# Layer 0 attention: products with v two steps behind their scores and between the halves of a step, scores in steps without items one head at a time

## The chip, the cores and the metric

The kernel runs on one core of one Trainium2 chip. The metric is the device time of one execution in microseconds. Engines are named as in the profile: PE is TensorE (PEld its weight loads), DVE VectorE, ACT ScalarE, POOL GpSimd, SP the queue that issues DMAs.

## The reference, cut to what matters

```python
x = L0_attn_x                                   # [2, 1024, 128]
xn = layernorm(x)
x = x + attn0(xn) + ffn0(xn)                    # layer 0
xn = layernorm(x)
x = x + attn1(xn) + ffn1(xn)                    # layer 1 (linear attention by chunks, gated LoRA)

def attn0(x):                                   # 16 heads of width 8
    q, k, v = split(x @ W_attn + b_attn)
    att = q @ k.T / sqrt(8)
    att = att + (tril(j - i) + causal) * slope[h]
    att = softmax(att)
    return (att @ v) @ W_proj + b_proj
```

Only the attention of layer 0 is touched by the change. Layer 1 follows it and takes the second half of the time.

## The kernel before, in words

The 2 x 16 heads of layer 0 are worked off in 8 groups of 4 heads (`GROUPS`, `GH = 4`). A group has 10 units (`UNITS`, `NU = 10`), so there are 80 steps (`NSTEP`); step s is unit u = s mod 10 of group n = s // 10. In what follows S0 to S3 are the scores of the four heads of a step, e0 to e3 their exponentials, A and B the items of the first and second half of a step, and pv(s) the products with v of step s.

A step's **scores** (`scores`, L706) are matmuls of the operands `k_op` and `q_op`, 55 rows deep, up to 512 columns wide. Even heads use the upper half of the rows of PE and odd heads the lower half. Each head's scores go into one of three PSUM banks in turn (`ST_BANKS = 3`), so S of a head waits until the exponential three heads earlier is done: S3 waits for e0 of its own step, S0 of the next step for e1, S1 for e2. ACT takes the **exponential** of each head (L1485) into `prob`, which has three slots, one for each step (`P_SLOTS`). On a step with a diagonal block (units 0, 1, 2, 3, 8, 9) POOL then clears the upper triangle (L1625). Then PE makes the **products with v** (`pv`, L724), four heads side by side in strips of 16 columns, into PSUM bank 7. Units 2 and 9 end an accumulation; ACT copies bank 7 to `yacc` (`acc`, L1474), and the pv of units 3 and 0 wait for that copy (`s_acc`). Units 1 and 8 have two segments (384 and 128 columns), units 2 and 9 only 256 columns.

Beside this stand the **items**, work for later groups, put into steps by `items_of_step`. A "max" item is a set of score matmuls without the maximum subtracted (L594, here called M), with a mask added in some of them (L608), whose row maxima DVE takes (L1174). Its matmuls are put beside those of the scores in the same half of a step (`scores_beside`), one in the upper, one in the lower half of the rows. Items use two rings of PSUM banks in turn, so an item waits until the one two before it has been used (`s_used`). Most steps have two max items, one in each half. Once in steps of units 1 and 5 the first half has a "turn" item (L690): PE transposes the maxima that POOL has split, ACT copies them (L1439), and SP moves them with four DMAs into `q_op` (L491). The turn at unit 1 serves the scores of unit 3 of the same group, the one at unit 5 those of unit 0 of the next. Behind the latter's DMAs the same queue loads the operands of the next but one group (`load_ops`, L483), which the max item in unit 9 needs. From step 70 on there are no max items left; steps 71, 72, 73 and 76 have one other item each, that of step 76 being the transposes of the second layer norm (L683).

The order is written out by hand for every engine, and each engine works strictly in that order. Before the change pv(s-1) stood at the end of step s on PE, and `acc(s-1)` at the end of step s on ACT.

Of the kernel before, what the change touches and what calls it, by code (L numbers as in the profile page):

```python
# [33 lines left out]
GH = 4  # L34
# [58 lines left out]
NSTEP = NU * len(GROUPS)  # L93
# [16 lines left out]
MAX_OF = [(p, r) for rs in (range(NR0), range(NR0, NR)) for p in range(PAIRS) for r in rs]  # L110
NPART = ROWS_AT[1] + 8 * TPS
P_SLOTS = 3
ST_BANKS = 3
OP_SLOTS = 3
FIRST_ITEMS = 17
# [70 lines left out]
def build(nc, x, w, wright, consts, alibi_q, alibi_k, masks, chosen, out):  # L186
    alibi_q, alibi_k, masks, chosen = (v.bitcast(BF16) for v in (alibi_q, alibi_k, masks, chosen))
    with ExitStack() as ctx:
# [353 lines left out]
        def _(pe):  # L542
# [150 lines left out]
            def scores(s, heads):  # L693
                n, u = divmod(s, NU)
                slot = n % OP_SLOTS
                if u in (0, 3) and heads[0] == 0:
                    pe.wait_ge(s_mop[n % 2][int(u == 3)], 16 * GH * (n // 2 + 1))
                for h in heads:
                    k = GH * s + h
                    if k >= ST_BANKS:  # L700
                        pe.wait_ge(s_exp, k - ST_BANKS + 1)
                at = 0
                for j, i0, nn in UNITS[u][1]:
                    for h in heads:
                        rows = rows_of(h, EXP_K)
                        last = mm(PS[:, (GH * s + h) % ST_BANKS, at:at + nn], k_op[rows, slot, h // 2, P * j:P * j + P],  # L706
                                  q_op[rows, slot, h // 2, P * i0:P * i0 + nn], start=True, stop=True, skip_group_check=True)
                        if at + nn == UNIT_W[u]:
                            last.then_inc(s_st, 1)
                    at += nn  # L710
# [62 lines left out]
                for part in range(2):  # L773
                    unit_b(k, part)
            pe.wait_ge(s_unit_used, len(UB))
            for s in range(NSTEP + 1):
                beside = items_of_step(s) if s < NSTEP else ()
                for half in range(2):
                    mine = (beside[:(len(beside) + 1) // 2], beside[(len(beside) + 1) // 2:])[half]
                    if s < NSTEP:  # L780
                        heads = range(GH // 2 * half, GH // 2 * (half + 1))
                        if mine and ITEMS[mine[0]][0] == "max":
                            scores_beside(s, heads, mine[0])
                            mine = mine[1:]
                        else:
                            scores(s, heads)
                    for k in mine:
                        item(k)
                if s:
                    pv(s - 1)  # L790


            pe.wait_ge(s_exp, GH * NSTEP)
            all_used(pe, len(ITEMS))
            pe.wait_ge(s_acc, 1 + 2 * len(GROUPS))
# [597 lines left out]
        def _(a):  # L1393
# [79 lines left out]
                        a.wait_ge(s_scr[n > 0], SCR_EACH)  # L1473
                    sca.copy(yacc[:, n, SPAN * half:SPAN * half + SPAN], PS[:, 7, :]).then_inc(s_acc, 1)  # L1474

            for s in range(NSTEP + 1):
                u = s % NU
                beside = items_of_step(s) if s < NSTEP else ()
                if P_SLOTS <= s < NSTEP:
                    a.wait_ge(s_pv, s - P_SLOTS + 1)  # L1480
                for half in range(2):
                    for h in range(GH // 2 * half, GH // 2 * (half + 1)) if s < NSTEP else ():
                        k = GH * s + h
                        a.wait_ge(s_st, k + 1)
                        sca.activation(prob[:, s % P_SLOTS, h, 0:UNIT_W[u]], PS[:, k % ST_BANKS, 0:UNIT_W[u]],  # L1485
                                       ACT.Exp).then_inc(s_exp, 1)
                    for k in (beside[:(len(beside) + 1) // 2], beside[(len(beside) + 1) // 2:])[half]:
                        item(k)
                if s:
                    acc(s - 1)  # L1490
                if s < NSPAN:
                    second(NSPAN + s)
            for i in SECOND:
# [290 lines left out]
```

## Time and profile before

| what | value |
| --- | --- |
| median of 3 runs | 516.56 us (514.7 to 519.3) |
| the profiled execution | 514.42 us, span 512.7 us |
| busy PE, DVE, ACT, POOL | 431.6, 343.4, 264.7, 197.2 us |
| steps of the loop | 44.6 us (first scores) to 291.9 us (last product with v) |
| mean granted clock of PE | 0.948 of full speed |

The profiled execution lies 2.1 us under the median. A busy share of PE is no measure of its limit, since its matmuls overlap; waits and the chain of what released what tell more.

### The profile page before, as it was taken

Reading aid. Unit: us, or ns where it says so; the run is one execution under the profiler, and the core shown is the slowest. Engines: PE = TensorE matmul, PEld = TensorE weight load, DVE = VectorE, ACT = ScalarE, POOL = GpSimd, SP = SyncE. Lnnn points to the kernel's source line nnn. Section 1 sums busy time; section 2 is a strip of 40 time slices with the busy share of each in tenths; the row PEclk is TensorE's granted clock in tenths of the full one; section 3 lists DMA queues with packets and bytes.
Section 4 is the critical chain, followed back from the end, with each engine's and each line's share of the span. In section 5 each row is a group of like instructions: output and inputs, shape, how many; then the busy total and the mean of one; then the engine's idle time right before and its main releaser. Section 6 shows DMA issues by size and latency. Waiting matters only on the chain.

```text
span 512.7 us, 10900 instructions
## 1 busy us (share of the span) xinstructions
PE 431.6 (84%) x4283; PEld 195.2 (38%) x4284; DVE 343.4 (67%) x604; ACT 264.7 (52%) x593; POOL 197.2 (38%) x285
## 2 busy tenths in 40 slices
PE   6797889898998989998886896955979888978995
PEld 3253223232332323332232252412536445544764
DVE  5868778878888788888825095648763783656351
ACT  1566387877776677768676412224523350434331
POOL 3013325353322304122220227465754846485340
PEclk9999699999999899999997598977999999999999
DMA  7543070524202020020000023211020302120000
GB/s 238 185 131 71 2 247 2 176 47 170 70 3 71 1 60 13 3 70 2 2 3 2 0 93 113 83 41 63 23 83 22 106 25 80 62 84 2 4 22 22
DMA packets 19095, 31.96 MB, mean 62 GB/s; under 512 B 2544, under 2 KB 7120, under 8 KB 18724
## 3 DMA queue, kind: packets, MB, share of 16 engines
q1 hardware_dynamic: 19044, 31.27, 19.0%
q8 instruction: 34, 0.56, 0.4%
q14 instruction: 17, 0.14, 0.1%
HBM read 13.23 MB, written 8.06 MB: 42 GB/s over the span
## 4 chain that ended last, share of the span: by engine, by line
PE 41%; DVE 27%; DMA 8%; ACT 7%; POOL 7%; issue 6%; SPq 3%; DVEq 0%; ACTq 0%; POOLq 0%
DVE pmax L1174 13%; PE PS L724 7%; PE PS L941 6%; PE PS L706 5%; PE PS L839 4%; ACT prob L1485 4%; DMA k_op<-k_scr 3%; DMA turned<-by_sin 3%; PE PS L594 3%; POOL qr L1646 3%; DVE by_sin L1321 2%; SPq L491 2%; DVE qr L1317 2%; PE PS L560 2%; PE PS L608 2%
## 5 line engine op out<-in xcount | busy, mean ns | idle before, releaser
L1174 DVE TENSOR_REDUCE pmax<-PS 128x8 f32<-128x1024 f32 x144 | 170.8, 1221 | 38.7 <-PE PS L608 29.7
L1485 ACT ACTIVATE prob<-PS 128x512 f32<-128x512 f32 (+1 forms) x320 | 158.2, 561 | 73.8 <-PE PS L706 72.6
L1625 POOL TENSOR_SCALAR_AFFINE_SELECT prob<-prob 128x512 f32<-128x512 f32 x64 | 39.9, 635 | 170.3 <-ACT prob L1485 170.3
L706 PE MATMUL PS<-q_op,k_op 55*128 55x512 bf16 (+3 forms) x384 | 93.3, 339 | 13.3 <-ACT prob L1485 10.0
L594 PE MATMUL PS<-k_op,q_op 52*128 52x512 bf16 (+3 forms) x384 | 78.9, 338 | 12.9 <-DVE pmax L1174 9.2
L724 PE MATMUL PS<-prob,vaug 128*16 128x512 f32 (+3 forms) x768 | 82.3, 518 | 1.4 <-ACT prob L1485 1.4
L839 PE MATMUL PS<-xnT,w_sb 128*128 128x512 f32 x80 | 45.8, 674 | 20.8 <-DVE by_sin L1321 20.8
L706 PEld LDWEIGHTS PS<-q_op,k_op 55*128 55x128 bf16 x384 | 26.1, 95 | 92.0 <-ACT prob L1485 74.7
L1354 DVE TENSOR_TENSOR state<-PS,xn 128x512 f32<-128x512 f32 x28 | 19.3, 691 | 54.6 <-PE PS L923 28.6
L1646 POOL TENSOR_TENSOR qr<-qr,turned 128x512 f32<-128x512 f32 x32 | 40.8, 1281 | 18.4 <-DMA turned<-by_sin 18.1
L1671 POOL TENSOR_TENSOR xn<-state,c_sb 128x512 f32<-128x512 f32 x28 | 29.1, 1041 | 41.7 <-DVE state L1354 33.5
L1552 ACT COPY oT<-PS 128x512 f32<-128x512 f32 x32 | 17.1, 587 | 39.7 <-PE PS L910 39.7
L594 PEld LDWEIGHTS PS<-k_op,q_op 52*128 52x128 bf16 x384 | 21.6, 94 | 31.1 <-DVE pmax L1174 22.4
L1517 ACT ACTIVATE vdec<-vk,c_sb 128x64 f32<-128x64 f32 x128 | 32.3, 335 | 0.5
L1506 ACT COPY vk<-PS 128x512 f32<-128x512 f32 x16 | 9.3, 584 | 42.3 <-PE PS L850 42.3
L941 PE MATMUL PS<-oT,w_sb 128*128 128x256 f32 (+1 forms) x160 | 29.2, 341 | 1.2 <-ACT oT L1552 1.2
L941 PEld LDWEIGHTS PS<-oT,w_sb 128*128 128x128 f32 x160 | 25.3, 191 | 6.7 <-issue 3.0
L1321 DVE TENSOR_TENSOR by_sin<-PS,c_sb 128x512 f32<-128x512 f32 x40 | 27.3, 681 | 0.0
L1317 DVE TENSOR_TENSOR qr<-PS,c_sb 128x512 f32<-128x512 f32 x32 | 21.9, 686 | 7.5 <-PE PS L839 7.5
L839 PEld LDWEIGHTS PS<-xnT,w_sb 128*128 128x128 f32 x80 | 13.3, 201 | 35.3 <-DVE by_sin L1321 24.6
L1328 DVE TENSOR_TENSOR sm<-PS,c_sb 128x512 f32<-128x512 f32 x32 | 20.5, 683 | 6.8 <-PE PS L868 6.8
L724 PEld LDWEIGHTS PS<-prob,vaug 128*16 128x16 f32 x768 | 14.7, 96 | 23.6 <-issue 13.6
(187 smaller groups left out, 552.3 us busy)
## 6 DMA issues: line engine op xcount, KB each, us to landing
turned<-by_sin SPq DMA_DIRECT2D x80, 128.0 KB, 2.0
k_op<-k_scr SPq DMA_DIRECT2D x14, 220.0 KB
q_op<-q_scr SPq DMA_DIRECT2D x14, 208.0 KB
c_sb<-const_dram SPq DMA_DIRECT2D x1, 2060.0 KB, 7.3
w_sb<-w_dram SPq DMA_DIRECT2D x1, 1876.5 KB, 7.6
q_scr<-part_a SPq DMA_DIRECT2D x6, 256.0 KB, 3.4
k_scr<-part_a SPq DMA_DIRECT2D x6, 256.0 KB, 3.7
q_scr<-part_b SPq DMA_DIRECT2D x6, 256.0 KB, 3.5
```

The costliest lines, as they stand in the source:

```text
L594: return mm(PS[:, ring + odd, P * at:P * (at + nb)], q_op[rows, slot, pair, P * i:P * i + P], k_op[rows, slot, pair, P * j:P * (j + nb)], ...
L706: last = mm(PS[:, (GH * s + h) % ST_BANKS, at:at + nn], k_op[rows, slot, h // 2, P * j:P * j + P], q_op[rows, slot, h // 2, P * i0:P * i0 ...
L724: last = mm(PS[STRIP * h:STRIP * h + VW, 7, c0:c0 + nn], vaug[:, TPB * b + j, g * GH + h, :], prob[:, s % P_SLOTS, h, at:at + nn], start=( ...
L839: mm(bank01(("p", i, m)), w, xnT[:, SPAN * i:SPAN * i + SPAN], start=True, stop=True).then_inc(s_pj, 1)
L941: last = mm(of_half(ps, s), wo[:, C * kt:C * kt + C], of_half(oT[:, i % 2, kt, :], s), start=False, stop=(chunks.stop == TPS and s == 1 an ...
L1174: vec.tensor_reduce(pmax[:, of_pair, at:at + TPS], both.rearrange("p a (b c) -> p a b c", c=P), AX.X, ALU.max).then_inc(done, 1)
L1317: note(vec.tensor_tensor(dst, ps, K["cos"][:, t], ALU.mult))
L1321: vec.tensor_tensor(by_sin[:, n % SIN_SLOTS, :], ps, K["sin"][:, t], ALU.mult).then_inc(free(("p", i, m)), 1)
L1485: sca.activation(prob[:, s % P_SLOTS, h, 0:UNIT_W[u]], PS[:, k % ST_BANKS, 0:UNIT_W[u]], ACT.Exp).then_inc(s_exp, 1)
L1517: sca.mul(vdec[:, c % 2, g, h % HPG, :], vk[:, c % 2, D1 * g:D1 * g + D1], K["kdec"][:, h:h + 1]).then_inc(s_vd_a, 1)
L1625: po.affine_select(out=blk, in_=blk, compare_op=ALU.is_ge, fill=0.0, base=0, pattern=[[0, GH], [1, P]], channel_multiplier=-1).then_inc(s_ ...
L1646: po.tensor_tensor(dst, dst, turned[:, n % TURN_SLOTS, :], ALU.add).then_inc(done, 1)
```

## The change

On PE the loop runs over `NSTEP + LAG` steps with `LAG = 2`. From step 2 on, pv(s-2) is issued in step s after the first half's scores and items and ahead of S2; after the last step pv(78) and pv(79) follow. On ACT `acc(s-2)` stands between e2 and e3 of step s. Where a half of a step has no max item at its head, its two heads are issued one after the other, each with its own wait for a bank, instead of both behind the wait for the later one.

```diff
+LAG = 2
@@ PE
-            for s in range(NSTEP + 1):
+            for s in range(NSTEP + LAG):
                 beside = items_of_step(s) if s < NSTEP else ()
                 for half in range(2):
+                    if half and s >= LAG:
+                        pv(s - LAG)
                     mine = (beside[:(len(beside) + 1) // 2], beside[(len(beside) + 1) // 2:])[half]
...
                         else:
-                            scores(s, heads)
+                            for h in heads:
+                                scores(s, [h])
                     for k in mine:
                         item(k)
-                if s:
-                    pv(s - 1)
@@ ACT
-            for s in range(NSTEP + 1):
+            for s in range(NSTEP + LAG):
...
                         sca.activation(prob[:, s % P_SLOTS, h, 0:UNIT_W[u]], PS[:, k % ST_BANKS, 0:UNIT_W[u]],
                                        ACT.Exp).then_inc(s_exp, 1)
+                        if s >= LAG and h == GH - 2:
+                            acc(s - LAG)
...
-                if s:
-                    acc(s - 1)
+                if s >= NSTEP:
+                    acc(s - LAG)
```

The new lines move line numbers by two on PE (L706 becomes L708, L724 L726) and by one on ACT (L1485 becomes L1486, L1474 L1475).

**Place 1, PE, from the end of step 10 to the second half of step 11**, before. L608 ends the items of step 10, L724 is a pv, L706 are scores, L690 is the turn:

```order
L608 MATMUL PS<-masks_sb 64x128 x4
L724 MATMUL PS<-prob,vaug 16x256 x4
L706 MATMUL PS<-q_op,k_op 128x384 x2
L706 MATMUL PS<-q_op,k_op 128x128 x2
L690 MATMUL PS<-masks_sb,mpart 12x128 x4
L706 MATMUL PS<-q_op,k_op 128x384
L706 MATMUL PS<-q_op,k_op 128x128
```

The same place now:

```order
L610 MATMUL PS<-masks_sb 64x128 x4
L708 MATMUL PS<-q_op,k_op 128x384
L708 MATMUL PS<-q_op,k_op 128x128
L708 MATMUL PS<-q_op,k_op 128x384
L708 MATMUL PS<-q_op,k_op 128x128
L692 MATMUL PS<-masks_sb,mpart 12x128 x4
L726 MATMUL PS<-prob,vaug 16x256 x4
L708 MATMUL PS<-q_op,k_op 128x384
```

pv(9) has moved from ahead of the step's scores to behind its turn item, and the two heads of the first half stand apart.

**Place 2, PE, from the second half of step 12 into step 13**, whose S0 waits for the DMAs of the turn (L594 are max items), before:

```order
L706 MATMUL PS<-q_op,k_op 128x256
L594 MATMUL PS<-k_op,q_op 128x512
L706 MATMUL PS<-q_op,k_op 128x256
L594 MATMUL PS<-k_op,q_op 128x512
L724 MATMUL PS<-prob,vaug 16x384 x4
L724 MATMUL PS<-prob,vaug 16x128 x4
L706 MATMUL PS<-q_op,k_op 128x512
```

The same place now:

```order
L708 MATMUL PS<-q_op,k_op 128x256
L596 MATMUL PS<-k_op,q_op 128x512
L708 MATMUL PS<-q_op,k_op 128x256
L596 MATMUL PS<-k_op,q_op 128x512
L708 MATMUL PS<-q_op,k_op 128x512
L596 MATMUL PS<-k_op,q_op 128x512
L708 MATMUL PS<-q_op,k_op 128x512
L596 MATMUL PS<-k_op,q_op 128x512
L610 MATMUL PS<-masks_sb 64x128 x4
L726 MATMUL PS<-prob,vaug 16x384 x4
L726 MATMUL PS<-prob,vaug 16x128 x4
```

pv(11) stood ahead of step 13's first scores and now stands behind them.

**Place 3, ACT, steps 13 and 14 and the start of 15** (L1485 exponentials, L1474 the copy to `yacc`), before, with the semaphores that each waits for:

```order
L1485 ACTIVATE prob<-PS 128x512 [waits s_st,s_pv]
L1485 ACTIVATE prob<-PS 128x512 [waits s_st] x3
L1474 COPY yacc<-PS 128x512 [waits s_pv]
L1485 ACTIVATE prob<-PS 128x512 [waits s_st,s_pv]
L1485 ACTIVATE prob<-PS 128x512 [waits s_st] x3
```

The same place now:

```order
L1486 ACTIVATE prob<-PS 128x512 [waits s_st,s_pv]
L1486 ACTIVATE prob<-PS 128x512 [waits s_st] x3
L1486 ACTIVATE prob<-PS 128x512 [waits s_st,s_pv]
L1486 ACTIVATE prob<-PS 128x512 [waits s_st] x2
L1475 COPY yacc<-PS 128x512 [waits s_pv]
L1486 ACTIVATE prob<-PS 128x512 [waits s_st]
```

The copy to `yacc` has moved three exponentials later, to between e2 and e3 of the next step.

## Rows read from the trace of the kernel before

**Rows 1.** The page: busy time by engine, granted clock in 40 slices, chain by engine

```profile
PE 431.6 (84%) x4283; PEld 195.2 (38%) x4284; DVE 343.4 (67%) x604; ACT 264.7 (52%) x593; POOL 197.2 (38%) x285
...
PEclk9999699999999899999997598977999999999999
...
PE 41%; DVE 27%; DMA 8%; ACT 7%; POOL 7%; issue 6%; SPq 3%; DVEq 0%; ACTq 0%; POOLq 0%
```

**Rows 2.** Busy time by stretch (window, its length, then engines, clock, DMA share, GB/s)

```profile
80.00:107.00 27.00, 24.07 (x242) 7.74 (x240) 22.17 (x22) 20.94 (x45) 12.83 (x29) 1.00 0.34 106
107.00:135.00 28.00, 25.64 (x250) 8.73 (x248) 24.10 (x22) 21.18 (x44) 11.26 (x25) 1.00 0.35 110
```

**Rows 3.** Who waited for whom, 44 to 292 us: total us, times, longest

```profile
DVE pmax L1174 <- PE PS L608: 26.0, 34, 2.3
...
PE PS L706 <- ACT prob L1485: 10.0, 23, 1.1
PE PS L594 <- DVE pmax L1174: 9.2, 21, 1.0
...
PE PS L706 <- DMA q_op<-mrow: 1.7, 3, 0.9
...
PE PS L594 <- DMA k_op<-k_scr: 1.6, 3, 1.0
```

**Rows 4.** Timeline of step 26 and the start of 27: start us, length us, engine, line

```profile
126.45 0.39 PE L706 MATMUL PS<-q_op,k_op 55*128 55x512 bf16 x1
...
126.94 2.06 ACT L1485 ACTIVATE prob<-PS 128x512 f32<-128x512 f32 x4 [1.00 <-PE PS L706]
127.13 2.36 DVE L1174 TENSOR_REDUCE pmax<-PS 128x8 f32<-128x1024 f32 x2 [0.31 <-PE PS L594]
...
127.59 0.39 PE L706 MATMUL PS<-q_op,k_op 55*128 55x512 bf16 x1 [0.31 <-ACT prob L1485]
...
127.91 0.25 PE L608 MATMUL PS<-masks_sb 64*64 64x128 bf16 x4
...
128.09 1.05 PE L724 MATMUL PS<-prob,vaug 128*16 128x512 f32 x8
...
129.07 0.39 PE L706 MATMUL PS<-q_op,k_op 55*128 55x512 bf16 x1
```

**Rows 5.** Chain that ended last, 79 to 108 us, in order of time

```profile
79.98 0.22 PE PS L594 x2
...
84.61 0.09 ACT yacc L1474
...
86.08 0.39 ACT mrow L1439
...
88.53 1.71 DMA q_op<-mrow
...
90.28 0.39 PE PS L706
...
96.74 0.45 ACT mrow L1439
...
101.29 5.41 DMA k_op<-k_scr
...
106.83 0.40 PE PS L594 x2
```

**Rows 6.** Timeline of the end of the loop, steps 76 to 78

```profile
275.92 1.94 PE L683 MATMUL PS<-w_sb,xn 128*128 128x128 f32 x8 [1.48 <-DVE xn L1062]
...
278.33 1.91 PE L724 MATMUL PS<-prob,vaug 128*16 128x512 f32 x8
...
280.17 0.61 PE L706 MATMUL PS<-q_op,k_op 55*128 55x512 bf16 x2
...
280.88 1.08 ACT L1485 ACTIVATE prob<-PS 128x512 f32<-128x512 f32 x2 [1.35 <-PE PS L706]
...
281.62 0.61 PE L706 MATMUL PS<-q_op,k_op 55*128 55x512 bf16 x2 [0.83 <-ACT prob L1485]
```

## The prediction

> **What bounds the kernel now.** I read the page first [rows 1]: no engine is full over the span, and the chain that ended last changes hands between PE, DVE, DMA and ACT. So the loop of layer 0 has to be read by what its steps wait for. Two stretches of one group each are 27 and 28 us long, with DVE busy 22.2 and 24.1 us, ACT 20.9 and 21.2, PE 24.1 and 25.6 [rows 2]. Nobody is full there either. The list of waits [rows 3] says where the slack sits: DVE waits 26.0 us for masked max items, PE waits 10.0 us for exponentials and 9.2 us for DVE, and a few waits are for DMAs.
>
> Then the timeline of a plain step [rows 4]. S0 is issued at 126.45, e0 starts at 126.94 (0.49 later), S3 is issued at 127.59 once e0 has freed its bank (0.65 after e0 began), pv follows at 128.09 (0.50 later, 0.18 of it the mask's four small matmuls) and the next S0 at 129.07 (0.98 later). 0.49 + 0.65 + 0.50 + 0.98 = 2.62 us, the whole step. So a plain step is a ring: S0, e0, S3, pv, next S0. DVE needs 2.36 us of it.
>
> Last the chain over a whole group [rows 5]. From the max item of step 9 (79.98) to the copy of the turn at unit 1 (end 86.47), its DMAs, S0 of unit 3 (90.28), the copy of the turn at unit 5 (end 97.19), its DMAs and behind them the loads of the operands, to the max item of step 19 (106.83). Two of its four links are DMAs: 90.28 - 86.47 = 3.8 us and 106.83 - 97.19 = 9.6 us. In this group PE waits for both.
>
> **The change part by part.**
>
> *pv between the halves.* It adds and removes no matmul. Draw the new ring of a plain step: S2 is now the head behind pv. S2 leads to e2, e2 frees the bank of S1 of the next step, behind S1 comes pv, behind pv the next S2. These are the same four links with the same durations [rows 4]: 0.49 + 0.65 + (0.32 or 0.50) + 0.98. With three banks, the head that leads and the head that waits are three apart wherever pv stands, so turning the order by half a step does not shorten the ring. What changes is whose mask lies in it: that of B before, of A after. B has masks in units 0, 6, 8, 9, A in 0, 2, 3, 9, with the turn steps (1 and 5) aside. Two plain steps gain 0.18 and two lose it: 0. The wait of PE for exponentials, 10.0 us [rows 3], therefore stays, at S1 instead of S3.
>
> *The lag of two.* pv(s-2) can never wait for its exponentials or triangles. Such waits are the PE rows before pv; they are not among the leading ones of [rows 3], and where they occur (end of units 2) the DMA wait of the next step follows at once. Gain 0, at most 1.5 us.
>
> *The two DMA links.* These do not turn with the order. I walk the group of [rows 5] again with the new order, in the durations of [rows 4]. Link 1, step 9 to the first copy: the pv of units 7 and 8 (0.98 each) now lie in it, before those of 8 and 9, of which 9 is half as wide (about 0.5). S1 of step 11 also waits for e2 of step 10, which has pv(8) ahead of its scores. e0 and e1 of step 11 then queue behind e2 and e3 of step 10, and the copy ends about 0.5 later than before. Link 2 is the DMA's 3.8, as before, but PE reaches it earlier and waits about 1.4 us, and pv(11), which used to be done ahead of this wait, now comes after it (place 2). Link 3, S0 of unit 3 to the second copy, was 97.19 - 90.28 = 6.9. ACT has 10 exponentials at 0.515 (2.06 for 4), the copy to `yacc` and the copy of the turn at some 0.55 each: 6.25 us, plus 0.49 to start. New is that e2 waits for pv(11): S1 0.22, S1 to pv with A's mask 0.50, pv 1.0, S2 to e2 0.49 makes 2.2 after S0, and e1 is done at 1.5. Idle 0.7, sum 7.4, so +0.5. Link 4, 9.6, is unchanged. The group is 1.0 longer.
>
> The others, by the same walk: the second group (28 us) starts DVE's stretch 1.4 later and gets back 0.6, since pv now fills PE's wait for DVE, and the turn's copy no longer stands in line: +0.8. In groups 3 and 4 DVE has more work, and the wait for DVE in the second half of a step is what pv now covers: 0 and -0.4. Group 5 is bound at both ends by the DMA links: +0.1. Group 6 is like the first up to unit 3, +0.9. At step 69 the turn waits for POOL, which waits for e3 of step 68. pv(66) now stands ahead of that, and pv(67) behind the turn: +0.5.
>
> *The end.* After the transposes of step 76 five pv were left; now six are. That stretch runs at half clock: the pv there takes 280.17 - 278.33 = 1.84 us instead of 0.98 [rows 1, 4, 6], so its move costs 0.9. The ring S0 280.17, e0 280.88, S3 281.62 [rows 6] turns like the plain one and keeps its length. One S alone ahead of pv gives back a little: +0.8 in all.
>
> *acc between e2 and e3.* Before, it stood ahead of e0, and e0 heads the ring: in [rows 5] it stands in the chain at 84.61. 16 copies at 0.2 to 0.4 would be 3 to 6 us if every ring were the bound. Behind e2 it is off the ring. I count nothing on top of the walk, which has it in place: the groups' lengths come from the DMA links, into the third of which it still falls. Its bound below zero is -5.
>
> *Scores singly.* They matter in the steps from 70 on and in the turn steps' first half. Two scores issued together overlap: the pair at 281.62 is 0.61 long [rows 6] where one is 0.39 at full clock [rows 4]. Issued singly, the first comes earlier, the second when the pair would have come. Only the second leads to pv, so 0. The bound, if each pair lost its overlap on the path: 36 pairs (20 in the last ten steps, 16 in turn steps) by at most 0.61 - 0.39 = 0.22, so 8 us.
>
> The Trainium skill speaks against this part ("TensorE: Matmul & The Clock Gate", "Part 3: Packing small matmuls"): tiles in different row groups run at the same time, so a pack takes little more than one matmul; one issued alone gives that up. By that rule alone the sum would be nearer its bound of 8 than nothing. The trace agrees on the overlap; that it lies on the path no row shows.
>
> **The sum**: 0 + 1.0 + 0.8 + 0 - 0.4 + 0.1 + 0.9 + 0.5 + 0.8 = +3.7 us. 514.4 becomes 518.1 in a profiled execution, and since that run lay 2.1 us under the median, 516.6 becomes 520.2.
>
> **The rivals.**
>
> *Faster: pv as cover.* PE's waits for DVE (9.2 us) fall mostly in second halves, where pv now stands ahead of them. If all of those are filled, and acc off the ring counts at its lower price (3), the time falls by 9 to 12: 507. For it: the 26.0 us that DVE stands idle. Against it: the DMA links, which no such gain shortens; it decides if the time from unit 5 to unit 9 and from unit 1 to unit 3 on PE stays above 9.6 and 3.8 us in most groups. Chance 0.19.
>
> *Only turned.* The DMA waits were small before (1.7 and 1.6 us, three times each [rows 3]); if the copies of the turns come no later than before, nothing is left but noise and the end: 516.6, give or take 2. Chance 0.22.
>
> *Slower: the copy gates pv.* pv of units 0 and 3 overwrites bank 7 and waits for acc. Before, a step lay between. Now acc waits its turn behind e2, in unit 1 behind the turn's copy too, and in my walk of the first group it ends 8.35 us after the max item of step 9, where pv(10) wants to start at 8.4. If ACT is later than that by more than 0.1 us, PE stops with S2 behind it, and the ring gets longer by the rest of the copy and a semaphore, some 0.5 us at 16 places: 8 us on top of part of the forecast, 526. Chance 0.14.
>
> *Slower: lost overlap* as above, with two thirds of its bound: 525. Chance 0.05. That the change does not do what it says is excluded by the order of instructions.
>
> **How the numbers follow.** The forecast has 0.40. A measurement of this kernel can tell about 1% from no change: 511.4 and 521.7 are the bounds. The faster rival lies below 511.4 with 0.15 of its 0.19, and 0.02 comes from the bound of acc: 0.17. Above 521.7 lie the two slower rivals with 0.17 and a third of the forecast with 0.12: 0.29. The rest, 0.54, is within 1%. For 8 in 10 the range leaves out most of the faster rival and the far end of the slower ones: 511 to 526.
>
> **What would show it.** In the profile after: the plain step keeps 2.44 to 2.62 us, with PE's wait for ACT now ahead of the scores that precede pv; PE's wait for the DMA `q_op<-mrow` grows from 1.7 to 5 us or more; its wait for `k_op<-k_scr` grows too; PE's wait for DVE falls from 9.2 to under 6; pv waits for nothing. If pv waits for the copy to `yacc`, the slower rival holds. If DVE's 26.0 us of waiting fall by a third, I was wrong on the links.

## The result and the profile after

The changed kernel took 525.3 us in the median of its first measurement, which takes in one execution of 928.3 us; the other three took 522.4, 523.5 and 527.1 us, with a median of 523.5. The kernel before took 515.6 (513.6 to 519.3). The recorded ratio is 1.0242, 95% interval [1.018, 1.0304]. Two later measurements of the same code gave 1.0133 [1.0067, 1.02] and 1.0186 [1.0131, 1.0242], with medians of 521.8 and 520.4 us. So the change makes the kernel slower, by 1 to 2.5% by these ratios, where I had put the largest chance on less than 1%. The ratios compare fast executions alone, those within about 1.5% of the fastest of their kernel, which takes away 40 of the 93 executions of the kernel before and none of the changed one's 18, so they come out higher than the ratio of the means over all executions, 521.4 to 516.4 us or 1.010. The execution of 928.3 us stands far apart from all others and is left out of every other figure; since it was the profiled one, the profile after comes from the second measurement.

**At equal clock.** Executions of one kernel differ by up to 17 us, and they differ with the mean granted clock of PE, which is recorded for each. A straight line through the 241 timed executions of all kernels of this study (one offset for each kernel, one common slope) falls by 3.4 us for each 0.01 of granted clock and leaves 1.6 us of scatter. The line is a correlation: it does not say whether the clock is a cause of the time or goes with it. Below, "at equal clock" is a kernel's value on that line at a clock of 0.94, with two standard errors. The kernel before has 517.5 ± 0.3 (93 executions, mean 516.4 at 0.943), the changed one 520.5 ± 0.8 (18 executions, mean 521.4 at 0.937). Of the 5.0 us between the means, 3.0 ± 0.8 are there at equal clock and 2.0 go with the clock. Through the 184 executions alone that the ratios use, the line falls by 2.8 us for each 0.01, and the difference is 4.4 instead of 3.0. The measurements were made on three chips; the four sets of executions of the kernel before lie at 517.4, 517.4, 517.5 and 517.9 us on the line, so the chip is no large part of any difference below.

The page of the changed kernel answers to [rows 1]. The chain has less of DVE in it (27% before) and more of PE and of DMA:

```profile
PE 436.9 (84%) x4283; PEld 198.1 (38%) x4284; DVE 342.1 (66%) x604; ACT 262.3 (50%) x593; POOL 197.4 (38%) x285
...
PEclk9998699999999999998877997967899999998999
...
PE 46%; DVE 19%; DMA 10%; ACT 8%; POOL 7%; issue 6%; SPq 4%; DVEq 0%; POOLq 0%; ACTq 0%
```

The windows of the first two groups, as in [rows 2] (the first is 1 us longer, the second 0.2 shorter by its first scores; the window is cut to whole us):

```profile
80.00:108.00 28.00, 24.01 (x244) 7.58 (x240) 22.43 (x21) 20.75 (x44) 13.55 (x33) 1.00 0.31 102
108.00:136.00 28.00, 25.30 (x255) 8.69 (x253) 24.29 (x23) 20.75 (x44) 11.39 (x26) 1.00 0.35 110
```

The waits of the loop, 44 to 305 us, as in [rows 3] (total us, times, longest):

```profile
DVE pmax L1175 <- PE PS L610: 27.9, 36, 2.6
...
PE PS L596 <- DVE pmax L1175: 7.0, 11, 1.3
...
PE PS L596 <- DMA k_op<-k_scr: 5.0, 4, 2.0
PE PS L692 <- POOL mpart L1605: 3.9, 2, 2.0
PE PS L708 <- ACT prob L1486: 3.9, 10, 0.6
PE PS L708 <- DMA q_op<-mrow: 3.1, 3, 1.3
PE PS L692 <- DVE pmax L1175: 3.1, 4, 1.1
```

Read this beside [rows 3]: PE waits 6.1 us less for exponentials and 2.2 less for DVE ahead of the max items, but 3.4 more for the loaded operands, 1.4 more for the DMAs of the turn, 1.1 more for DVE ahead of the turn and 3.9 for POOL's `mpart`, where before had 0.8. What was won in front of the engines came back in front of the DMAs and the turn.

A plain step, as in [rows 4]:

```profile
127.06 0.39 PE L708 MATMUL PS<-q_op,k_op 55*128 55x512 bf16 x1
...
127.48 2.06 ACT L1486 ACTIVATE prob<-PS 128x512 f32<-128x512 f32 x4 [0.31 <-PE PS L708]
...
127.78 0.39 PE L708 MATMUL PS<-q_op,k_op 55*128 55x512 bf16 x1
...
128.21 0.38 PE L708 MATMUL PS<-q_op,k_op 55*128 55x512 bf16 x1
...
128.52 1.05 PE L726 MATMUL PS<-prob,vaug 128*16 128x512 f32 x8
...
129.50 0.39 PE L708 MATMUL PS<-q_op,k_op 55*128 55x512 bf16 x1
```

From 127.06, the head behind one pv, to 129.50, the head behind the next, is 2.44 us, and PE does not stop for more than a gap of issue before the pv. The next such stretch, in the step with two segments, is 2.38 us. The ring has turned and kept its length within 0.1 us. But PE does not wait for an exponential in these steps at all. Before step 70 its waits for exponentials ahead of scores fell from 4.3 us in all to 0.5; the other 3.4 of the 3.9 us above are in the last ten steps.

The chain over the first group, as in [rows 5]:

```profile
85.51 0.42 ACT mrow L1440
...
88.00 1.71 DMA q_op<-mrow
...
89.76 0.39 PE PS L708
...
96.40 0.40 ACT mrow L1440
...
100.90 5.45 DMA k_op<-k_scr
...
106.48 0.40 PE PS L596 x2
```

The first max item of step 9 (78.29, before 79.70) to the end of the first copy (85.93, before 86.46) is 7.6 us (6.8 before), copy to S0 of unit 3 is 3.8 (3.8), S0 to the end of the second copy at 96.80 is 7.0 (6.9), and from there to the max item of step 19 it is 9.7 (9.6). The end of the loop, as in [rows 6]:

```profile
280.21 1.94 PE L685 MATMUL PS<-w_sb,xn 128*128 128x128 f32 x8 [0.65 <-DVE xn L1063]
...
282.08 1.67 PE L726 MATMUL PS<-prob,vaug 128*16 128x512 f32 x8
...
284.76 0.39 PE L708 MATMUL PS<-q_op,k_op 55*128 55x512 bf16 x1 [0.47 <-ACT prob L1486]
285.08 1.05 PE L726 MATMUL PS<-prob,vaug 128*16 128x512 f32 x8
```

From the first scores to the end of the last product with v the loop is 2.2 us longer in this profile (249.5 us against 247.3), and layer 1, whose code is the same, 6.7 (227.5 against 220.8). The latter is no effect of the change that a profile can show: in the sixteen profiles of the experiments layer 1 took 223.8 to 230.3 us, with 27 to 42 us of it at half clock, and the profile of before, with 22.8 us at half clock, was the shortest of all. Lengths of the loop are comparable only with their time at half clock beside them: 30.4 us before, 34.1 after. The profile of the third measurement of the changed kernel has a loop of 247.5 us, also with 34.1 at half clock. So single profiles put the loss in the loop anywhere from 0.2 to 2.2 us.

### The profile page after: what moved, and what is told of

Read it like the earlier page. It is cut to its first block, busy times and chain, and to the rows that moved or that the text cites. A ratio compares the mean times of both kernels' runs of the same rounds, so it can differ in the third digit from the quotient of the medians.

```text
span 926.6 us, 10862 instructions
## 1 busy us (share of the span) xinstructions
PE 904.5 (98%) x4284; PEld 318.7 (34%) x4284; DVE 347.5 (38%) x604; ACT 277.8 (30%) x593; POOL 200.5 (22%) x285
## 4 chain that ended last, share of the span: by engine, by line
PE 95%; DVE 2%; ACT 1%; DMA 1%; issue 0%; POOL 0%; SPq 0%; POOLq 0%
PE PS L726 19%; PE PS L840 11%; PE PS L708 10%; PE PS L942 8%; PE PS L596 8%; PE PS L911 4%; PE PS L869 4%; PE PS L924 4%; PE PS L893 4%; PE PS L639 2%; PE PS L848 2%; PE PS L610 2%; DVE pmax L1175 2%; PE PS L562 2%; PE PS L756 1%; PE PS L764 1%
## 5 line engine op out<-in xcount | busy, mean ns | idle before, releaser
L1486 ACT ACTIVATE prob<-PS 128x512 f32<-128x512 f32 (+1 forms) x320 | 168.9, 558 | 220.9 <-PE PS L708 217.7
L726 PE MATMUL PS<-prob,vaug 128*16 128x512 f32 (+3 forms) x768 | 181.4, 1038 | 0.0
L708 PE MATMUL PS<-q_op,k_op 55*128 55x512 bf16 (+3 forms) x384 | 168.7, 591 | 1.9 <-ACT prob L1486 0.8
L596 PE MATMUL PS<-k_op,q_op 52*128 52x512 bf16 (+3 forms) x384 | 152.8, 599 | 3.3 <-DVE pmax L1175 1.6
L840 PE MATMUL PS<-xnT,w_sb 128*128 128x512 f32 x80 | 102.3, 1419 | 0.0
L708 PEld LDWEIGHTS PS<-q_op,k_op 55*128 55x128 bf16 x384 | 32.3, 112 | 177.8 <-issue 132.9
L942 PE MATMUL PS<-oT,w_sb 128*128 128x256 f32 (+1 forms) x160 | 77.6, 716 | 1.2 <-ACT oT L1555 1.2
L924 PE MATMUL PS<-vdec,vk 64*64 64x256 f32 x240 | 43.5, 826 | 0.0
L869 PE MATMUL PS<-qr,kr 64*64 64x256 f32 x256 | 41.1, 807 | 2.4 <-POOL qr L1649 2.4
L893 PE MATMUL PS<-sm,vk 64*64 64x256 f32 x256 | 42.6, 819 | 0.0
L911 PEld LDWEIGHTS PS<-qd,state 64*64 64x64 f32 x960 | 37.9, 279 | 11.3 <-issue 9.7
L726 PEld LDWEIGHTS PS<-prob,vaug 128*16 128x16 f32 x768 | 22.3, 112 | 54.6 <-issue 27.8
L911 PE MATMUL PS<-qd,state 64*64 64x64 f32 x960 | 40.8, 374 | 0.1
```

Source lines behind the costliest of these rows:

```text
L596: return mm(PS[:, ring + odd, P * at:P * (at + nb)], q_op[rows, slot, pair, P * i:P * i + P], k_op[rows, slot, pair, P * j:P * (j + nb)], ...
L726: last = mm(PS[STRIP * h:STRIP * h + VW, 7, c0:c0 + nn], vaug[:, TPB * b + j, g * GH + h, :], prob[:, s % P_SLOTS, h, at:at + nn], start=( ...
L840: mm(bank01(("p", i, m)), w, xnT[:, SPAN * i:SPAN * i + SPAN], start=True, stop=True).then_inc(s_pj, 1)
L869: last = mm(PS[half_of(s), 2 + q, 256 * pr:256 * pr + 256].rearrange("p (a t) -> p a t", a=HPG), kr[rows, i % 2, pr, t], qr[rows, i % 2, H ...
L893: last = mm(PS[out_rows(s, q), 4 + s, at], vk[half_of(s), c % 2, D1 * g:D1 * g + D1], sm[half_of(s), 2 * (c % 2) + q, at], start=(pr == 0) ...
L911: last = mm(PS[out_rows(s, q), 4 + s, D1 * k:D1 * k + D1], state[rows, (2 * c + s) % STATES, k, :], qd[rows, c % 2, k, half_of(s)], start= ...
```

## The experiments

Before each stands its edit, against the kernel before or the changed one ("after"). The table has every measurement; mean clock, median and value at equal clock are over all executions but that of 928.3 us, and the row "before" has all 93 executions of that kernel, while each ratio was taken against those beside it.

| kernel | median us | ratio to before [95%] | mean clock | at equal clock |
| --- | --- | --- | --- | --- |
| before | 516.9 | 1 | 0.943 | 517.5 ± 0.3 |
| after, 1st measurement | 523.5 | 1.0242 [1.018, 1.0304] | 0.932 | 521.6 ± 1.8 |
| after, 2nd measurement | 521.8 | 1.0133 [1.0067, 1.02] | 0.937 | 520.0 ± 1.1 |
| after, 3rd measurement | 520.4 | 1.0186 [1.0131, 1.0242] | 0.941 | 520.8 ± 1.3 |
| after, scores in pairs | 522.2 | 1.0065 [1.0027, 1.0102] | 0.938 | 522.4 ± 0.9 |
| before, scores singly | 516.6 | 0.9971 [0.9938, 1.0005] | 0.943 | 517.6 ± 0.9 |
| before, lag 2 at step end | 514.3 | 0.9966 [0.9928, 1.0004] | 0.943 | 516.4 ± 0.9 |
| after, lag 1 and pairs | 552.4 | 1.0646 [1.0593, 1.0698] | 0.923 | 546.3 ± 1.4 |
| before, early loads | 512.8 | 0.9943 [0.9906, 0.9981] | 0.950 | 515.7 ± 1.0 |
| after, early loads | 518.3 | 1.0072 [1.0037, 1.0107] | 0.934 | 516.3 ± 1.0 |
| after, acc at step end | 521.2 | 1.0125 [1.007, 1.0181] | 0.943 | 521.9 ± 1.3 |
| after, split first | 518.6 | 1.0094 [1.0035, 1.0154] | 0.941 | 519.1 ± 0.9 |
| after, split first, early loads | 515.8 | 1.005 [1.0007, 1.0094] | 0.944 | 517.5 ± 0.9 |
| before, split first | 525.2 | 1.013 [1.0073, 1.0187] | 0.939 | 525.2 ± 1.3 |
| after, pv(67) ahead of turn | 520.4 | 1.0139 [1.0068, 1.021] | 0.944 | 521.1 ± 1.3 |
| after, pv ahead of all turns | 519.9 | 1.015 [1.0082, 1.0218] | 0.946 | 520.7 ± 1.3 |
| after, early loads, early turn | 513.5 | 1.0034 [0.9998, 1.007] | 0.946 | 515.4 ± 0.9 |
| before, four edits | 508.3 | 0.9829 [0.9769, 0.989] | 0.949 | 512.9 ± 1.3 |

**The changed kernel again**, with no edit, and once more beside the last experiments:

> The changed kernel unchanged, for a second measurement beside the variants and for a profile of an ordinary execution. The four times so far put it about 12 us over the kernel before (ratio 1.024), where I forecast 4. Links theory (the DMAs of the turns and loads bound each group, and each group gets about 1 us longer): PE's waits for the DMA q_op<-mrow 5 us or more in all, mean clock as before (0.948). Gate theory (pv of units 0 and 3 waits for the copy to yacc): pv rows show ACT yacc as releaser, 5 to 8 us in all. Clock theory (more of the loop at half clock): the waits grow little, the granted clock is 0.94 or less, and the stretches that are longer are those at half clock.

> The changed kernel unchanged, third measurement: ratio 1.01 to 1.02, the same waits as in its first profile within 0.3 us each, half clock from about 255 to 266 again, and about 520 us at a clock of 0.94.

Both were slower than before by more than 1% in their intervals' middle, and both show the same waits (`q_op<-mrow` 3.1 us and `mpart` 3.9 in each, `k_op<-k_scr` 5.0 and 4.5). Two of the texts' forecasts missed: the wait for `q_op<-mrow` was to be 5 us or more, and the half clock from 255 to 266 did not come back in the third measurement. No pv row names `yacc` for more than 0.2 us, against the gate theory. The clock of 0.937 and 0.941 is what the clock theory said, though it had the waits growing little.

**Scores in pairs again, in the changed order; and scores singly alone in the old order.**

```diff
-for h in heads: scores(s, [h])
+scores(s, heads)
```

> The changed kernel with the two heads of a half issued together again where no max item stands at its head (one part of the change undone). Lost-overlap theory: this takes back most of the 12 us, so within 3 us of the kernel before. Links and gate theories: nothing changes against the changed kernel, within 2 us.

```diff
-scores(s, heads)
+for h in heads: scores(s, [h])
```

> The kernel before with only the scores of such halves issued one head at a time. Lost-overlap theory: slower by 5 to 8 us. Links, gate and clock theories: within 2 us of the kernel before.

Alone in the old order the single scores cost nothing (0.9971; 517.6 ± 0.9 at equal clock against 517.5), though they took PE's wait for exponentials from 10.0 to 6.6 us. In the changed order with pairs that wait is the largest of PE:

```profile
PE PS L708 <- ACT prob L1485: 14.6, 27, 0.8
```

against 3.9 with singles. Where these waits are matters: 6.3 us are in the turn steps and 7.5 in the last ten, each time ahead of a pair that starts a step, and only 0.7 in all other steps, where before had 4.3. So the new place took the waits for exponentials out of the plain steps and put them in front of pairs, and the singles took those away again. At equal clock pairs cost 1.9 ± 1.2 us there (522.4 against 520.5; 0.8 ± 1.2 on the line through 184 executions, so this is not firm); the medians of the direct comparison (522.2 and 521.8) cannot show so little. No run speaks for a loss from the missing overlap.

**The lag of two alone**, pv(s-2) and acc(s-2) at the end of step s in the kernel before; **and the place between the halves with a lag of one.**

```diff
-if s: pv(s - 1)
+if s >= LAG: pv(s - LAG)     # and acc likewise, on ACT
```

> The kernel before with the lag alone: pv(s-2) and acc(s-2) at the end of step s, scores joint. Measured so far, at equal clock: changed kernel +2.6 us, lag of one between the halves +29 us, scores singly alone 0. Position theory (between the halves a lag of one makes pv wait for the exponentials just made; with a lag of two the place costs little): the lag alone at the end of the step is neutral or gains up to 2 us, since pv no longer waits for POOL after units 1 and 8. Links theory: it turns the order by a whole step, which puts one step's pv more behind the links; within 2 us of the kernel before.

```diff
-LAG = 2
+LAG = 1
...
+scores(s, heads)
```

> The changed kernel with a lag of one instead of two and joint scores: pv of the last step between the halves, acc between e2 and e3. The order on PE is no longer turned by half a step against the copies and DMAs but comes earlier by a step. Links theory: pv(9), pv(10) and pv(11) stand again as many as before between the links; near the kernel before, plus 0 to 3 us, since pv may now wait for its exponentials and triangles. Gate theory: as slow as the changed kernel or slower, since the copy still stands behind e2. Position theory (between the halves is bad in itself): as the changed kernel.

The lag alone is free or slightly good (0.9966, 1.1 ± 1.0 us less at equal clock). The place between the halves with a lag of one costs 6%, 29 us at equal clock, where each theory had it near the kernel before or the changed one. The waits of PE in the loop say why:

```profile
PE PS L726 <- POOL prob L1627: 17.7, 22, 1.5
PE PS L708 <- ACT prob L1485: 13.5, 23, 0.8
PE PS L726 <- ACT prob L1485: 10.6, 18, 0.9
```

pv then waits 28.3 us for its own triangles and exponentials, against 0.7 us for anything with the lag of two. The lag is what makes the place possible.

**What the place alone costs.** Two pairs of kernels in the table differ in nothing but where pv and acc stand, both with a lag of two. With scores in pairs, "after, scores in pairs" is 6.0 ± 1.3 us over "before, lag 2 at step end" at equal clock. With single scores, early loads and the split first, "after, split first, early loads" is 4.6 ± 1.6 over "before, four edits". So the loss of the change lies in the place. The change as a whole is then -1.1 (lag) + 6.0 (place, in pairs) - 1.9 (singles in the new place) = +3.0 us at equal clock.

**Early loads.** On SP the loads of the next but one group's operands are issued ahead of the turn's first DMAs instead of behind the last ones, so that `k_op` no longer comes after the turn of unit 5. In before and in after:

```diff
+if n + 1 < len(GROUPS): load_ops(n + 1)
 load_m(n, 0)
```

> The kernel before with the loads of a group's operands (L483) issued ahead of the DMAs of the turn at unit 5 instead of behind them, so that the link of 9.6 us is gone. Links theory: PE's wait for k_op<-k_scr (1.6 us) goes to 0 and the time falls by 1 to 3 us. If the link does not bind, nothing changes.

> The same edit in the changed kernel, where PE waited 5.0 us for k_op<-k_scr. Links theory: it gains more than the same edit in the kernel before, by 2 to 5 us, and comes out level with or ahead of the kernel before. If the changed kernel still trails the edited kernel before by 2.6 us or more at equal clock, the loads' link is not where the change loses.

In both, the wait for `k_op<-k_scr` is gone from the list. It brings 1.8 ± 1.0 us in the kernel before and 4.2 ± 1.3 in the changed one, at equal clock. That is the test of this link: it holds 2.4 ± 1.6 us more in the changed order. With it loosened in both, 0.6 ± 1.4 of the 3.0 us remain. What is left to wait for on PE in that changed kernel:

```profile
PE PS L596 <- DVE pmax L1175: 7.7, 13, 1.2
...
PE PS L708 <- DMA q_op<-mrow: 2.8, 3, 1.2
```

**acc at the end of the step, in after.** It puts the copy to `yacc` behind e3, to see how close the gate of the slower rival was:

```diff
-if s >= LAG and h == GH - 2: acc(s - LAG)
...
+if s >= LAG: acc(s - LAG)
```

> The changed kernel with the copy to yacc after e3 of the step instead of between e2 and e3. Gate theory (the copy behind e2 delays pv of units 0 and 3): no rows show pv waiting for the copy, so none of it left to gain; now the copy stands ahead of e0 as before. If the copy off the ring was worth something, this is 1 to 4 us slower than the changed kernel; if the copy's place costs nothing, the same within 1 us.

Now pv does wait for the copy, for which the changed kernel has one wait of 0.2 us:

```profile
PE PS L726 <- ACT yacc L1475: 2.7, 7, 0.7
```

7 times with 0.4 us each, where the rival had 16 times 0.5. The time is 1.4 ± 1.5 us longer at equal clock, which cannot be told from nothing or from the whole wait.

**Split first.** In the changed kernel's step 69 the turn waits for POOL, which makes `mpart` only after the three triangles of the step before. The timeline there, POOL and PE:

```profile
253.00 1.22 POOL L1628 TENSOR_SCALAR_AFFINE_SELECT prob<-prob 128x512 f32<-128x512 f32 x2 [2.86 <-ACT prob L1486]
...
255.42 0.25 POOL L1605 CAST mpart<-rleft 128x16 bf16<-128x16 f32 x1
...
255.81 0.33 PE L692 MATMUL PS<-masks_sb,mpart 128*12 128x128 bf16 x3 [1.87 <-POOL mpart L1605]
...
256.03 1.86 PE L726 MATMUL PS<-prob,vaug 128*16 128x512 f32 x5
```

The same wait, 2.0 us, stands at step 2. The edit puts POOL's splitting ahead of a step's triangles, in after, in after with early loads, and in before:

```diff
+split_at(s)
 for j, i0, nn in UNITS[s % NU][1]:   # triangles of the step
...
-split_at(s)
```

> The changed kernel with POOL splitting the maxima (L1601 to L1605) ahead of the step's triangles instead of behind them. In every profile with pv between the halves and a lag of two, PE waits 1.8 us at step 69 and 2.0 at step 2 for that split, and its clock falls to half within a us of the first of these waits, which no profile of the other kernels shows there. Clock theory (the wait takes the clock down): the wait at step 69 falls to 0.7 or less, the stretch at half clock from 255 on goes or shrinks, and the time falls by 3 to 6 us. If the wait goes but the stretch stays: 1 to 3 us. Links theory alone: 1 us.

> The changed kernel with both the split first and the operand loads ahead of the turn's DMAs. Links and clock theories together: what the change lost (2.6 us at equal clock and 1 to 3 by its clock) is gone, so level with or up to 4 us ahead of the kernel before; 3 to 5 us ahead of the changed kernel at least. If it still trails the kernel before, something else costs.

> The kernel before with the split first, as the control of the first of these runs. PE waited only 0.8 us for POOL's split there, and its clock was full at step 69. Clock and links theories: within 1.5 us of the kernel before. If it gains as much as the changed kernel does, the split's place is no part of what the change lost.

In after the waits for `mpart` are gone, and so is the stretch at half clock behind them:

```profile
255.00:266.00 11.00, 9.51 (x65) 3.35 (x66) 1.99 (x4) 7.09 (x16) 3.61 (x9) 1.00 0.01 3
```

The time falls by 1.4 ± 1.2 us at equal clock. That measure takes out what the clock gives back; the mean falls from 521.4 to 518.7, by 2.7, still under the 3 to 6 of the clock theory. Together with the early loads the gains do not add: 517.5 at equal clock where the early loads alone had 516.3. In before the same edit costs 7.7 ± 1.3 us, where both theories had it within 1.5 us of the kernel before, since with a lag of one the pv now waits for the triangles that were pushed back:

```profile
PE PS L724 <- POOL prob L1626: 8.2, 7, 2.1
```

The profile of before has no such row. It prices what the lag of two buys: freedom for POOL.

**pv ahead of the turn.** The other way to fill the wait at step 69: pv(67) ahead of the turn item of that step alone, and then pv ahead of the turn item in all 16 steps that have one.

```diff
+if half == 0 and s == 69: pv(s - LAG)            # first kernel, in short
+if half == 0 and "turn" in kinds: pv(s - LAG)    # second kernel, in short
 for k in mine:
     item(k)
```

> The changed kernel with one pv moved: in step 69 pv(67) stands ahead of the turn item instead of behind it, so that PE works while POOL splits. Clock theory (that wait starts the half-clock stretch): the wait falls from 1.8 to 0.9 us or less, the stretch from 255 to 266 is gone or starts later and is shorter, the time falls by 1 us and up to 5 with the clock. If the stretch stays, the wait is not what starts it, and the gain is 1 us at most.

> The changed kernel with pv ahead of the turn item in all 16 steps that have one. Waits of PE for POOL and DVE before L692 (3.9 and 3.1 us) fall to under 2 in all. But each turn's copy comes up to 1 us later, so where the links bind, the DMA waits grow: links theory says gain in the waits and loss in the links cancel, within 2 us of the one before. If the links do not bind it is 3 to 6 us faster than the changed kernel.

The first halves the wait at step 69 (1.87 to 0.90 us), and its window from 255 to 266 us is at full clock:

```profile
255.00:266.00 11.00, 8.57 (x61) 2.65 (x59) 1.54 (x3) 5.97 (x15) 3.66 (x9) 1.00 0.01 4
```

The time shows nothing of it at equal clock (521.1 ± 1.3); the mean is 519.8 us against 521.4. The second takes the waits for `mpart` and gives them to the copy's DMAs:

```profile
PE PS L708 <- DMA q_op<-mrow: 4.5, 3, 2.0
...
PE PS L692 <- POOL mpart L1607: 1.1, 2, 0.9
```

A pv ahead of the turn makes the turn's copy later, and its DMAs pass it on to S0 of unit 3. The time at equal clock stays (520.7 ± 1.3). Here the wait was filled with work that stands ahead of the next link of the same chain, and nothing was won.

**Both DMA links loosened.** Early loads, and the splitting and turn of unit 1 one item earlier, so that its four DMAs are issued sooner:

```diff
+if n + 1 < len(GROUPS): load_ops(n + 1)
...
-if n and u == 3:
+if n and u == 2:
```

> The changed kernel with the loads early and the turn at unit 1 one item earlier (in unit 0), so that its DMAs have one step more. Links theory: PE's wait for q_op<-mrow (2.8 us with the loads early) falls to under 1, and the time by 1 to 3 us against the run with the loads early alone (516.3 at a clock of 0.94).

```profile
PE PS L596 <- DVE pmax L1175: 9.0, 14, 1.2
PE PS L692 <- POOL mpart L1605: 5.0, 2, 3.2
PE PS L708 <- ACT prob L1486: 3.3, 9, 0.6
```

PE's waits for the DMAs of both links are down to 0.6 us (`q_op<-mrow`), and the kernel is 5.1 ± 1.2 us below the changed one at equal clock: 515.4 ± 0.9, level with before and its early loads, 515.7 ± 1.0. The step from the early loads alone (516.3) is 0.9 ± 1.4, so the early turn by itself is not told from nothing. This does not show that the place costs nothing once the links are loosened. Before with its early loads has a lag of one and scores in pairs, and the early turn was not tried in it, though with 0.7 us of waiting for `q_op<-mrow` it had little to win. The pair of kernels with equal lag, singles and early loads still puts 4.6 ± 1.6 us on the place.

**The parts that did no harm, together, without the place:** the kernel before with the lag of two at the step's end, single scores, early loads and split first.

> What helped or did no harm, on the kernel before: pv and acc with a lag of two but at the end of the step, scores singly, loads early, split first. Sum of the parts at equal clock: -1.0 + 0 - 1.8 - about 0.5; 3 to 5 us faster than the kernel before.

508.3 us, 0.9829 [0.9769, 0.989]; 512.9 ± 1.3 at equal clock, 4.6 us less than before. With the lag of two, POOL can split first (with a lag of one that alone was +7.7), and the pv stays at the end of the step. It beats both kernels. Against "after, split first, early loads", from which it differs only in the place of pv and acc, PE's waits changed like this; first that kernel, then this one:

```profile
PE PS L596 <- DVE pmax L1175: 8.3, 14, 1.2
...
PE PS L708 <- DMA q_op<-mrow: 3.1, 2, 1.8
PE PS L726 <- POOL prob L1629: 2.5, 4, 0.7
```

```profile
PE PS L596 <- DVE pmax L1175: 7.0, 15, 1.0
...
PE PS L708 <- DMA q_op<-mrow: 1.4, 2, 0.7
```

The waits for the turn's DMAs and for POOL are where the place still costs once the loads are early; with pv at the step's end the second list has no wait of pv for POOL. Which share each of its four edits has was only tried for three of them: -1.1 for the lag, 0 for the singles, -1.8 for the loads, together -2.9 of the 4.6.

## Where the prediction was right, and the step that failed

*The ring.* Right in its length: 2.44 and 2.38 us from head to head, beside the forecast's lower end of 2.44 to 2.62.

*PE's wait for exponentials "therefore stays".* Wrong. Before step 70, outside the turn steps, it fell from 4.3 us to 0.5 with singles and 0.7 with pairs: the ring kept its length, but PE no longer stood still in it. The 14.6 us of the pairs are in the turn steps and the last ten. I had counted the singles at nothing either way. They were worth about -1.9 in the new order and nothing in the old. The bound of +8 us for the lost overlap was far off; the runs show no such cost. It also rested on a misreading: the pair of 0.61 us stood at half clock and the single one of 0.39 at full clock. At full clock a pair takes 0.39 too (first row, before), and at half clock a single one 0.60 (second row, after):

```profile
270.21 0.39 PE L706 MATMUL PS<-q_op,k_op 55*128 55x512 bf16 x2 [1.08 <-ACT prob L1485]
```

```profile
278.96 0.60 PE L708 MATMUL PS<-q_op,k_op 55*128 55x512 bf16 x1 [0.26 <-ACT prob L1486]
```

The Trainium skill's rule ("TensorE: Matmul & The Clock Gate", "Part 3: Packing small matmuls"), by which the sum would have been near that bound, is borne out by the traces as to the overlap, not as to the time.

*The lag of two.* Right: pv waits for almost nothing (0.7 us), and the lag alone is 1.1 ± 1.0 us less where I had said 0 to -1.5.

*The two DMA links.* Right in kind for the loads, and an experiment shows it and not only the profile: loosening them brought 4.2 us in the changed order and 1.8 in the old. For the turn's DMAs the waits show it, and no time does. The place costs 4.6 ± 1.6 us with the loads early as well, so the loads' link is not all of its cost. In detail, from the first scores of each group: group 1 +1.0 (forecast +1.0), group 2 -0.2 (+0.8), group 3 -0.8 (0), group 4 -0.9 (-0.4), group 5 -1.5 (+0.1), group 6 +4.1 (+1.4 with step 69). Within group 1, link 1 was 0.9 longer and not 0.5, link 3 0.1 and not 0.5, links 2 and 4 were unchanged. PE's wait for `q_op<-mrow` grew to 3.1 us and not to 5, that for `k_op<-k_scr` from 1.6 to 5.0, that for DVE fell to 7.0 and not below 6. Groups 2 to 5 gave back 4.0 us more than I had allowed. This fits the faster rival's pv as cover (PE's waits for DVE and for exponentials did fall), but no run isolates it.

*Step 69.* Forecast +0.5, measured 1.3 by the wait (1.87 us against 0.55). Much of the rest of group 6's +4.1 is half clock: steps 65 and 69 took 5.5 and 4.4 us in this profile against 3.8 and 2.4 before, and the profile of the third measurement, at full clock there, had the group 1.6 longer and not 4.1.

*The end.* +1.0 (forecast +0.8), and +1.9 in the profile of the third measurement, with more half clock there.

*acc.* Whether its place off the ring brings anything is not shown (1.4 ± 1.5 us). At the end of the step it does gate pv, 2.7 us in 7 places. So "the copy gates pv" did not happen but was near, as the walk of the first group had said.

*The sum.* +3.7 by the terms, 3.0 ± 0.8 measured at equal clock. That they agree is partly luck. By part, the place was forecast at +3.7 and measured at 6.0 ± 1.3, the lag at 0 and -1.1 ± 1.0, the singles at 0 and -1.9 ± 1.2; by group, misses of -4.0 and of +2.7 stood against each other. **The step that failed is how I went from this sum to the time**: "514.4 becomes 518.1 in a profiled execution, and since that run lay 2.1 us under the median, 516.6 becomes 520.2". The terms were priced at the clock of their rows, full clock except at the end, and the clock itself was taken to be what it was. It was not: over 18 executions of the changed code the granted clock is 0.006 ± 0.004 lower than over 93 of the old, which is 2 us by the slope. In the first three it was 0.932, which is 3.8 us by the slope, so that 516.4 + 3.0 + 3.8 = 523.2 stands beside their mean of 524.3. The recorded ratio of 1.024 is higher still than these three against the four listed values of before (524.3 to 516.0, or 1.016). Part of the verdict is thus which executions were drawn: over all of them the change is +5.0 us or 1.0%, a third more than forecast. With +3.7 us or 0.7% before it, the forecast lay 1.5 us from the bound of 1%, and two more put it across. The chance for "slower" was too small for that, a third of the forecast's 0.40.

*What stays open* is why the clock is lower, and whether it is more than the draw of executions. The trace shows half-clock stretches that come and go between executions of one kernel. Windows from 255 to 266 us, around and behind step 69's wait, in before, in the second measurement of after and in the third:

```profile
255.00:266.00 11.00, 8.93 (x80) 3.13 (x76) 1.86 (x3) 7.85 (x18) 3.76 (x9) 1.00 0.01 4
```

```profile
255.00:266.00 11.00, 9.88 (x42) 2.65 (x42) 0.00 (x0) 4.32 (x9) 1.79 (x5) 0.55 0.01 2
```

```profile
255.00:266.00 11.00, 9.43 (x76) 3.41 (x76) 1.79 (x3) 7.47 (x17) 3.14 (x5) 1.00 0.01 3
```

The second window, at 0.55, does 42 matmuls in the time of 80 and 76. I took the 1.87 us wait at step 69 for what starts that stretch. The third window is of the same code with the same wait and runs at full clock, so the wait alone does not decide it. But all profiles together say more. Seven have that wait of 1.87 us at step 69 (after twice, its pairs, early loads, acc at step end, early turn, lag 1 and pairs), and in five of them the granted clock falls from full to half (2.4 to 1.2 GHz) 0.3 to 1.3 us after PE resumes and stays there for 10.2 us. None of the other ten has a low stretch there. The six of them with a lag of two have 30.7 or 34.1 us at half clock in the whole loop; the four kernels with pv between the halves in which the wait is gone or halved have 23.9 each, though before, without the wait, has 30.4. The mean clock of those four is 0.943 over 36 executions, that of the kernels of the six 0.939 over 58, and that of before 0.943. So the low stretch goes with the wait in these profiles, and the wait is not enough for it. Its share of the time is small, 0.004 of clock or 1.3 us by the slope, and whether it is the cause is not shown.

## What to carry to other kernels

When an order is turned around a ring of equal links, look for the links that do not turn with it: chains through DMAs with a fixed length, whose start moves with the work put ahead of them. Price a move by the latest of those, and test it by loosening the link in both orders. Test the move by a pair of kernels that differ in nothing else; a comparison in which lag, pairing and place change together can look level while the place costs 4.6 to 6.0 us. When the sum is under 1% and a clock wanders from execution to execution, give the clock a term and a range of its own before the sign of the result is called, and do not judge a theory of the clock at equal clock.

## What the runs showed of the hardware that I had not expected

One execution of the changed kernel took 928.3 us. Its page and its pv row:

```profile
PE 904.5 (98%) x4284; PEld 318.7 (34%) x4284; DVE 347.5 (38%) x604; ACT 277.8 (30%) x593; POOL 200.5 (22%) x285
...
L726 PE MATMUL PS<-prob,vaug 128*16 128x512 f32 (+3 forms) x768 | 181.4, 1038 | 0.0
```

A pv matmul takes 1038 ns in the mean there where the second profile has 515, and the other engines are busy at most 6% longer (ACT 277.8 us against 262.3). The clock given for this execution, 1.00, is no reading: of the eighteen profiles its page alone has no PEclk row, since its trace holds no record of the granted clock. So a low clock is not excluded, but half clock alone would not do. A row of eight pv matmuls:

```profile
215.86 2.42 PE L726 MATMUL PS<-prob,vaug 128*16 128x512 f32 x8
```

Such a row takes 1.05 us at full clock [rows 4] and 1.91 at half clock [rows 6]. PE was slower here than at either level that the other traces show, all through the run. It came once in some 240 executions, and what it was stays open.

Second, the slope: 0.01 of mean granted clock goes with 3.4 us, or 0.65%, of this kernel, and single executions of the kernel before span 0.923 to 0.968. That is 15 us of the 17 that they differ by.
